# An attention kernel on one core: where the values of images 2 and 3 are projected, and who sends half of the first group's maxima

## What is computed

```python
qkv = xw.reshape(Bw, N, C) @ qkv_w + qkv_b
q, k, v = (qkv[0], qkv[1], qkv[2])
attn = jnp.einsum('bhnd,bhmd->bhnm', q * scale, k)
rel_h = jnp.einsum('bnhwc,hkc->bnhwk', rq, Rh)
rel_w = jnp.einsum('bnhwc,wkc->bnhwk', rq, Rw)
attn = (attn.reshape(Bw, NH, WS, WS, WS, WS) + rel_h[..., :, None] + rel_w[..., None, :]).reshape(Bw, NH, N, N)
attn = jax.nn.softmax(attn, axis=-1)
out = jnp.einsum('bhnm,bhmd->bhnd', attn, v)
```

## Time and profile before

| what | value |
|---|---|
| runs of before | 407.2, 411.94, 412.54 us (median 411.94) |
| the profiled execution's own time | 412.37 us |
| its span, first to last instruction | 410.5 us |
| PE (TensorE) busy | 364.2 us, 89% |
| DVE (VectorE) busy | 198.4 us, 48% |
| ACT (ScalarE) busy | 148.2 us, 36% |
| POOL (GpSimd) busy | 98.3 us, 24% |
| mean granted TensorE clock | 0.983 of full speed |
| chain that ended last | PE 70%, DVE 9%, issue 7%, ACT 6%, DMA 3%, SyncE's queue 2% |

### The profile page before, as it was taken

One profiled execution on the slowest core, in us unless ns is written; L12 is line 12 of the kernel. 1 busy time (PEld: TensorE's weight loads), 2 busy tenths in 40 slices (PEclk: granted clock), 3 DMA queues, 4 the chain that ended last, 5 costly groups with the idle time before them and its releaser, 6 DMA issues.

```text
span 410.5 us, 10402 instructions
## 1 busy us (share of the span) xinstructions
PE 364.2 (89%) x4462; PEld 267.4 (65%) x4462; DVE 198.4 (48%) x459; ACT 148.2 (36%) x322; POOL 98.3 (24%) x180
## 2 busy tenths in 40 slices
PE   5999698888887799999899688888887879999996
PEld 3477576667664449879567576667775437976656
DVE  6154667566736301327752657666756220151372
ACT  2085144443534540130167044443434263021220
POOL 2311338522332063000040408732232003000000
PEclk9799999999999999999999899999999899999999
DMA  7950000000020111100201000000000000000002
GB/s 227 334 164 11 3 3 6 2 4 4 2 104 2 30 24 73 57 0 2 77 2 30 2 2 2 4 2 4 5 2 2 0 2 0 0 2 0 2 0 77
DMA packets 8430, 13.01 MB, mean 32 GB/s; under 512 B 3041, under 2 KB 5922, under 8 KB 8386
## 3 DMA queue, kind: packets, MB, share of 16 engines
q1 hardware_dynamic: 8386, 12.37, 9.8%
HBM read 10.94 MB, written 0.79 MB: 29 GB/s over the span
## 4 chain that ended last, share of the span: by engine, by line
PE 70%; DVE 9%; issue 7%; ACT 6%; DMA 3%; SPq 2%; POOL 2%; POOLq 0%; DVEq 0%
PE banks L807 13%; PE banks L787 11%; PE banks L897 8%; PE banks L876 7%; DVE negmax L1295 4%; PE banks L678 3%; PE banks L707 3%; PE banks L820 3%; PE banks L750 3%; PE banks L1057 2%; PE banks L986 2%; PE banks L996 2%; PE banks L910 2%; ACT arena L1134 2%; PE banks L667 2%
## 5 line engine op out<-in xcount | busy, mean ns | idle before, releaser
L1134 ACT ACTIVATE arena<-banks 128x392 f32<-128x392 f32 (+2 forms) x144 | 58.7, 494 | 101.4 <-PE banks L807 101.4
L1295 DVE TENSOR_REDUCE negmax<-banks 128x4 f32<-128x784 f32 x48 | 46.4, 974 | 29.5 <-PE banks L787 27.1
L629 POOL TENSOR_TENSOR attention_arena<-o_and_sums,inverse_sums 128x196 f32<-128x196 f32 (+2 forms) x36 | 19.9, 551 | 100.5 <-DVE inverse_sums L1323 100.5
L876 PE MATMUL banks<-yT,fc 128*128 128x512 f32 (+1 forms) x96 | 35.7, 631 | 5.7 <-ACT yT L1082 5.7
L787 PE MATMUL banks<-attention_arena 32*128 32x196 f32 x384 | 29.4, 375 | 12.8 <-DVE negmax L1295 9.3
L820 PE MATMUL banks<-arena,v_and_ones 128*32 128x196 f32 (+2 forms) x672 | 30.9, 307 | 2.7 <-ACT arena L1134 2.7
L807 PE MATMUL banks<-attention_arena 32*128 32x196 f32 x384 | 26.5, 342 | 6.7 <-DMA attention_arena<-negmaxT 3.2
L897 PEld LDWEIGHTS banks<-fc,arena 128*128 128x128 f32 x192 | 31.1, 190 | 1.5 <-ACT arena L1152 1.5
L897 PE MATMUL banks<-fc,arena 128*128 128x192 f32 x192 | 31.7, 327 | 0.0
L787 PEld LDWEIGHTS banks<-attention_arena 32*128 32x128 f32 x384 | 15.6, 186 | 23.1 <-DVE negmax L1295 16.7
L876 PEld LDWEIGHTS banks<-yT,fc 128*128 128x128 f32 (+1 forms) x96 | 13.2, 195 | 24.6 <-issue 15.6
(11 more groups left out here) (157 smaller groups left out, 626.5 us busy)
## 6 DMA issues: line engine op xcount, KB each, us to landing
fc<-in_fc SPq DMA_DIRECT2D x2, 768.0 KB, 5.5
qkv<-in_qkv SPq DMA_DIRECT2D x2, 576.0 KB, 4.3
fc<-in_fc SPq DMA_DIRECT2D x2, 576.0 KB, 5.7
attention_arena<-negmaxT SPq DMA_DIRECT2D x72, 1.0 KB
rel<-in_rel SPq DMA_DIRECT2D x2, 448.0 KB, 4.9
x_tok<-in_x SPq DMA_DIRECT2D x4, 192.0 KB, 3.2
inverse<-in_inverse SPq DMA_DIRECT2D x1, 768.0 KB
edge_rel<-negmaxT SPq DMA_DIRECT2D x48, 0.5 KB
```

The lines of the kernel that those rows point to most:

```text
L629: pool.tensor_tensor(dst, shape(m.o[:, ring]), shape(m.inverse[:, ring]), ALU.mult).then_inc(s.weighed, 1)
L876: ins = mm(m.bank[j % 8][:, :], wl["fc1"][rows, half, 128 * hid:128 * (hid + 1)], m.yT[rows, half, 512 * g:512 * (g + 1)], start=not short ...
L1134: run(m.probsT[:, n % P_RING, j, 0:cols], m.bank[4 + j][:, 0:cols], ACT.Exp).then_inc(s.probs, 1)
L1295: dve.tensor_reduce(at[:, 0:8].rearrange("k (j a) -> k a j", a=2)[:, part], m.banks[:, bank0:bank0 + 4, 0:MAIN_KEYS], AX, ALU.max, negate= ...
```

## The change

It does four things.

1. The `v` jobs of images 2 and 3 leave their place behind images 0 and 1 and become the last two jobs of `PROJ`, in banks 2 and 3. `project_values` now does two images. TensorE computes them behind pieces 0 and 1, and ScalarE takes them out behind the load of the exponential's table.
2. The pieces ahead of `turn(0)` are four instead of five, with banks by `FIRST_BANK = (0, 4, 4, 0)`. Piece 3 now waits until ScalarE has taken the values of image 3 out of bank 3.
3. Piece 4 is computed right behind `turn(0)`, ahead of piece 5.
4. Of group 0's four DMAs with maxima SyncE issues two, and ScalarE the other two, behind its values.

```diff
-PROJ += [("v", n, 0, "act") for n in range(IMAGES)] + [("v_edge", n, 0, "act") for n in range(2)]
+PROJ += [("v", n, 0, "act") for n in range(2)] + [("v_edge", n, 0, "act") for n in range(2)]
 PROJ += [("rel_w", n, 0, "act") for n in range(SIDE // 2)] + [("rel_h", n, 0, "dve") for n in range(SIDE // 2)]
+PROJ += [("v", n, 0, "act") for n in range(2, IMAGES)]
...
-    return (4 + j) % 8
+    return PROJ[j][1] if PROJ[j][0] == "v" and PROJ[j][1] >= 2 else (4 + j) % 8
...
-FIRST_PIECES = PIECES.index((AHEAD, 0)) + 1
+FIRST_PIECES = PIECES.index((AHEAD, 0))
+FIRST_BANK = (0, 4, 4, 0)
...
-    return 4 * (i % 2) if i < FIRST_PIECES else 0
+    return FIRST_BANK[i] if i < FIRST_PIECES else 0
...
-    return i - 1 if i < FIRST_PIECES else i
+    return max([k + 1 for k in range(i) if piece_bank(k) == piece_bank(i)], default=0)
...
-                    for block in range(4):
...
+                    for block in range(2 if n == 0 else 4):
+                        sp.dma_start(*max_rows(n, block)).then_inc(s.max_rows[n % M_RING], 16)
...
-            def project_values(l):
+            def project_values(l, image):
...
+                for j in range(first, first + 2):
+                    if image == 0:
+                        bank = open_bank(s, j)
+                    else:
+                        pe.wait_ge(s.max, 1)
+                        bank = m.bank[job_bank(j)]
...
-                project_values(l)
+                project_values(l, 0)
                 project(l, job("v_edge", 0, 0), job("v_edge", 1, 0) + 1)
...
-                for i in range(FIRST_PIECES):
-                    score(l, i)
+                score(l, 0)
+                score(l, 1)
+                project_values(l, 2)
+                score(l, 2)
+                wait_for(pe, s.proj_in, *taken_out(job("v", 3, 0)))
+                score(l, 3)
 
                 pe.wait_ge(v_ones_set, 2)
-                wait_for(pe, s.proj_in, *taken_out(job("v_edge", 1, 0)))
                 for n in range(N_GROUPS):
                     turn(l, n)
+                    if n == 0:
+                        score(l, FIRST_PIECES)
...
+                act.wait_ge(s.edge_inputs, R_EDGES)
+                act.wait_ge(s.maxT, 1)
+                for block in range(2, 4):
+                    act.dma_start(*max_rows(0, block)).then_inc(s.max_rows[0], 16)
...
-                for i in range(FIRST_PIECES):
+                for i in range(FIRST_PIECES + 1):
                     take_max(i)
```

More of the change, by code:

```diff
@@ L483, in values_of, with max_rows @@
             return m.v[:, at, 4 * slot + j]
+        def max_rows(n, block):
+            slot, b = GROUPS[n]
+            lo, src = 32 * block, m.negmaxT[:, n % M_RING, :]
+            if b >= IMAGES:
+                return m.edgeR[MAX_ROW::GROUP, slot, b - IMAGES, lo:lo + 32], src[lo:lo + 4]
+            dst = m.r[MAX_ROW::GROUP, slot, PLACES * b:PLACES * (b + 1)].rearrange("j (a q) -> j a q", a=2)[:, :, lo:lo + 32]
+            src = src[lo:lo + 8]
+            return (dst, src) if block < 3 else (dst[:, 0], src[::2])
         def wait_for(eng, st, who, n):
@@ L556, in _ @@
                 sp.wait_ge(s.edge_inputs, R_EDGES)
[L557 removed]
+                for n in range(N_GROUPS):
                     sp.wait_ge(s.maxT, n + 1)
[L559 to L568 removed]
+                    for block in range(2 if n == 0 else 4):
+                        sp.dma_start(*max_rows(n, block)).then_inc(s.max_rows[n % M_RING], 16)
             out_dram = out.rearrange("b h w c -> b (h w) c").rearrange("b (t p) c -> b p t c", p=128)
@@ L716, in project @@
                             ins.then_inc(s.proj_in.pe, 1)
-            def project_values(l):
+            def project_values(l, image):
                 s, wl = A[l], w[l]
-                first = job("v", 0, 0)
-                for j in range(first, first + IMAGES):
-                    bank = open_bank(s, j)
+                first = job("v", image, 0)
+                for j in range(first, first + 2):
[4 more added lines that the diff above has]
+                        bank = m.bank[job_bank(j)]
                     for tile in range(2):
-                        at = 128 * (2 * (j - first) + tile)
+                        at = PLACES * PROJ[j][1] + 128 * tile
                         mm(bank[:, CH * tile:CH * (tile + 1)], m.yT[:, j % 2, at:at + 128], wl["qkv"][:, j % 2, 2 * CH:3 * CH],
                            start=tile == 0, stop=False, skip_group_check=True)
-                for pair in range(first, first + IMAGES, 2):
-                    for tile in range(2):
-                        for j in (pair, pair + 1):
-                            rows, at = rest_rows(j), 128 * (2 * (j - first) + tile)
-                            ins = mm(m.bank[job_bank(j)][:, CH * tile:CH * (tile + 1)], m.yT[rows, 1 - j % 2, at:at + 128],
-                                     wl["qkv"][rows, 1 - j % 2, 2 * CH:3 * CH], start=False, stop=True, skip_group_check=True)
-                            if tile == 1:
-                                ins.then_inc(s.proj_in.pe, 1)
+                for tile in range(2):
+                    for j in (first, first + 1):
+                        rows, at = rest_rows(j), PLACES * PROJ[j][1] + 128 * tile
+                        ins = mm(m.bank[job_bank(j)][:, CH * tile:CH * (tile + 1)], m.yT[rows, 1 - j % 2, at:at + 128],
+                                 wl["qkv"][rows, 1 - j % 2, 2 * CH:3 * CH], start=False, stop=True, skip_group_check=True)
+                        if tile == 1:
+                            ins.then_inc(s.proj_in.pe, 1)
             def relate(l, j):
@@ L836, in attention @@
                 project(l, 0, 2 * CHUNKS)
-                project_values(l)
+                project_values(l, 0)
                 project(l, job("v_edge", 0, 0), job("v_edge", 1, 0) + 1)
-                for j in range(job("rel_w", 0, 0), len(PROJ)):
+                for j in range(job("rel_w", 0, 0), job("v", 2, 0)):
                     relate(l, j)
-                for i in range(FIRST_PIECES):
-                    score(l, i)
+                score(l, 0)
[4 more added lines that the diff above has]
+                score(l, 3)
                 pe.wait_ge(v_ones_set, 2)
-                wait_for(pe, s.proj_in, *taken_out(job("v_edge", 1, 0)))
                 for n in range(N_GROUPS):
                     turn(l, n)
+                    if n == 0:
+                        score(l, FIRST_PIECES)
                     if n + AHEAD < N_GROUPS:
```

10 lines of the change are left out of this document (removed).

## The result

The changed kernel takes 413.2 us (median of 20 runs, 411.05 to 418.17) against 411.13 us of the kernel before (20 runs beside it, 406.78 to 413.95). The ratio is 1.0109, 95% interval 1.0083 to 1.0136: slower by about 1%, half of the 2% that the prediction called no difference. The medians lie 2.1 us apart, the ratio stands for 4.5 us (3.4 to 5.6). The forecast was 414.3 us, +2.4 us. A later run beside other kernels gave +2.6 us by medians and a ratio of 1.0068 (1.0027 to 1.0109).

What follows compares the result with a forecast made beforehand. The prediction took TensorE, busy 89% of the span, to bound the kernel through its order and waits. Terms summed to +1.15 us (attention 0) and +1.25 us (attention 1): 411.94 + 2.4 = 414.3 us, range 409.5 to 418.0 us.

Steps and rivals of the forecast that it cites:

- Values leave the front: Ahead of the relative positions: with half the values gone, piece 0 starts 1.43 us earlier in each attention block.
- Piece 0 to `turn(0)`: Stretch from piece 0 to turn(0): it grows by 0.57 us in attention 0 and 0.67 us in attention 1.
- ScalarE sends its first at T + 5.17: Ahead of turn(0): ScalarE's first DMA goes out behind its values, 5.17 us after piece 0 starts (T); an issue takes 0.59 us.
- rival of dear issues: ScalarE's DMAs ahead of turn(0): an issue costs 1.16 us rather than 0.59, giving 416.5 us; chance 0.15.
- Piece 4 behind `turn(0)`: Between turn(0) and turn(1): three pieces now wait in turn for maxima, one more link, +2.01 us in each block.
- The clock: At turn(0) of attention 1 or the new sparse stretch: the 1.67 us fall stays or moves there, nothing in the sum.
- More falls: New sparse stretches between the turns: further clock falls, 416.0 us with one more; chance 0.10.
- Rival 4: Ahead of turn(0): rows land early, turn(0) starts about 6.4 us after piece 0, total 412.3 us; chance 0.05.
- Trainium skill's rule: Group 0's DMAs: several issuing engines save only issue time, by itself about 1.2 us per attention block; not used in the terms.

Runs made afterwards that it cites:

- e7: Changed kernel with four extra, never-read matmuls in each of the two waits between turn(0) and turn(1); +1.0 us against the kernel before, ratio 1.0008.
- e1: Changed kernel with piece 4 put back ahead of turn(0); -1.3 us by medians against the kernel before, ratio 0.9970.
- e2: Changed kernel with all four DMAs of group 0 issued by SyncE again; +1.9 us against the kernel before, ratio 1.0068.
- e3: Changed kernel with ScalarE's two DMAs ahead of its two values instead of behind them; +2.9 us against the kernel before, ratio 1.0080.
- e4: Changed kernel with eight extra, never-read matmuls in each of the two waits between turn(0) and turn(1); +3.4 us against the kernel before, ratio 1.0108.
- g1: Changed kernel with moved values behind piece 3, piece 4 ahead of turn(0), and SyncE issuing all DMAs; -1.4 us against the kernel before, ratio 0.9981.
- e5: Changed kernel with piece 4 back ahead of turn(0) and all four DMAs by SyncE; -1.7 us against the kernel before, ratio 1.0025.
- f1: Kernel before with only piece 4 moved behind turn(0); +8.6 us against the kernel before, ratio 1.0235.
- c1: The changed kernel timed again, nothing altered, beside other kernels; +2.6 us against the kernel before, ratio 1.0068.

## Why the prediction was right, and where it was not

The forecast, 414.3 us and slower by less than 2%, held; the measured 413.2 us lies in its range. That the two lie 1.1 us apart is in part luck. The forecast stood on a median of three runs, 411.94 us, where 20 runs give 411.13, and one term of the sum, the clock, was missing. The range itself, 409.5 to 418.0 us, doesn't follow from the numbers named for it, which give 411.0 - 4.7 = 406.3 to 416.5 + 0.6 = 417.1. By its steps:

1. *Values leave the front: -1.43 us each.* Right, -1.37 and -1.36. The bound was not TensorE's queue but VectorE's last take-out. `relate` started 0.15 us behind it (24.16 against 23.27 + 0.74), where 0.05 was counted; ScalarE was not late, its first `rel_w` waited 0.18 us for TensorE.
2. *Piece 0 to `turn(0)`: +0.57 and +0.67 us.* Measured +0.66 and +0.23. The step "ScalarE sends its first at T + 5.17" was wrong twice in opposite ways. ScalarE issues while the first of its two values is still being taken out:

```profile
40.06 0.49 ACT L1122 ACTIVATE v_and_ones<-banks 128x384 f32<-128x384 f32 x1 [7.78 <-PE banks L739]
40.16 1.12 ACTq L1135 DMA_DIRECT2D attention_arena<-negmaxT  x1
40.45 0.48 ACT L1122 ACTIVATE v_and_ones<-banks 128x384 f32<-128x384 f32 x1
...
41.31 0.54 ACTq L1135 DMA_DIRECT2D attention_arena<-negmaxT  x1
```

The first issue is at T + 4.67, half a microsecond early, but it takes 1.12 us in attention 0 and 0.56 in attention 1, where 0.59 was taken for both. The second starts at T + 5.82 and T + 5.27, against T + 5.76 in the forecast. The rival of dear issues was thus true of one issue in the whole program.

3. *Piece 4 behind `turn(0)`: +2.01 us each.* Right and the largest term: e7 gives 2.12 us at the full clock, and e1 shows that without it the loss goes.
4. *The clock: "I take it that the fall stays or moves there, so nothing in the sum".* This is the step that failed. It moved there in attention 1 and came anew in attention 0: 1.65 + 1.41 - 1.67 = +1.4 us. The prediction named the sparse stretch, with about 1.2 us idle ahead of two of its pieces, and then gave it one fall in all instead of one in each attention, because attention 0 had shown none before. "More falls" was given 0.10.

The terms as measured: 2 x (-1.37) + 0.66 + 0.23 + 2 x 2.12 + 1.4 = +3.8 us. That lies between the two measures of the time (+2.1 and +4.5). The same count from the table, against before's 26.32 us in the four stretches, gives -1.1 for e1, +3.0 for e2 and e3, +3.9 for e4, +0.7 for e7, -1.1 for g1 and e5; their medians are -1.3, +1.9 and +2.9, +3.4, +1.0, -1.4 and -1.7. For f1 it gives +12.1 where the medians give +8.6; the profiled execution itself took 12.6 us more than before's median, and its six executions differ by their clock, as shown above.

Rival 4, rows as early as two saved issues allow, was rightly doubted: even with the DMAs ahead of the values (e3) `turn(0)` came no earlier than T + 6.6, and the time was no better.

The sentence on the Trainium skill's rule that several issuing engines save only issue time ("DMA: Bandwidth & Descriptors", "Issuing engines are not separate DMA queues") can now be set beside a measurement. It speaks of the issue time alone, and the two issues saved on SyncE, 0.59 us each, gained nothing here, since ScalarE's two stand behind its values: with SyncE alone `turn(0)` starts 0.65 and 0.23 us earlier (e2).

Open: why both fc1 starts fell in the profiles of the changed kernel, c1, e2 and e3, and only one or none in the others. It would add 1.7 us to the changed kernel's time, and nothing in its code near fc1 differs. It is not so in each execution: 5 of the 20 of the changed kernel have a mean clock of 0.992, which the two falls between the turns use up.

## What to carry to other kernels

Before filling a wait of the busiest engine, look at what already stands there: here piece 4 used it for nothing, and putting it behind the wait cost a link of 2.12 us, more than the 1.37 us that the filling won. A chain of short matmuls that wait for VectorE had a second price here, the clock: count the idle time of the stretch you make, and if one copy of it may draw a fall, reckon with one in each copy. To learn which of the two you pay, put useless matmuls into the waits, no longer than the wait: the chain stayed here, and the clock's share went.

## What the runs showed of the hardware that I had not expected

- Two waits of 1.14 to 1.18 us, with one piece of 0.94 us between them, brought the granted clock to its lower level ahead of the third piece in 8 of 8 profiled stretches, and four extra matmuls (1.15 us) in each of the two waits kept it at 1.00 in 2 of 2. In e1, where two waits of 1.18 us have 3.1 us of matmuls between them, it stayed at 1.00 in 2 of 2, and a single wait of 1.15 us between two turns (before's attention 0) left it there too. One wait of 2.90 or 2.81 us (f1) brought it down in 2 of 2; one of 1.65 us in attention 0 of before didn't, and one of 1.56 us in attention 1 did.
- The first DMA that ScalarE issues in the program takes 1.11 to 1.13 us (changed, c1, e1, e4, e7), the next ones 0.53 to 0.56 us. In e3 the first two together took 1.94 us and the two of attention 1 together 1.12 us. What makes the first one dear wasn't tried.
- ScalarE issues a DMA that stands behind two activations 0.10 us after the first of them starts (40.16 against 40.06 us), before the second starts (40.45) and well before it ends (40.93). The DMA doesn't read what they write.
- The first six qkv records, ahead of everything that any of these kernels changes, took 5.49 us in the profile of before, 2.84 in that of the changed kernel and 4.30 in that of c1. The granted clock over them was 0.50, 1.00 and 0.66, so this is the clock too. It alone makes 2.65 us between executions, as much as the effect studied, and is why spans of single profiles (410.5 and 413.0 us) say so little here.
